# Rounding constant taken off on ScalarE, value bias added on TensorE, and two result buffers in a quantised attention stage

## What is computed

```python
def _dyn_quant(x):
    s = jnp.maximum(jnp.max(jnp.abs(x), axis=-1, keepdims=True) / 127.0, EPS)
    q = jnp.clip(jnp.round(x / s), -127.0, 127.0)
    return (q, s)
def _w8a8_linear(x, w, b):
    qx, sx = _dyn_quant(x)
    qw, sw = _quant_weight(w)
    y = jnp.einsum('bnc,oc->bno', qx, qw) * (sx * sw[:, 0])
    return y + b
...
q = _w8a8_linear(x, wq, bq)          # per head
k = (cond @ wk.T + bk)
v = (cond @ wv.T + bv)
scores = q k^T * inv_sqrt_d + mask
o = softmax(scores) @ v
return _w8a8_linear(o, wo, bo)
```

## Time and profile before

| | |
|---|---|
| runs | 4305.97, 4312.45, 4316.20 us; median 4312.45 |
| the profiled execution | 4308.22 us; span 4306.5 us; mean granted TensorE clock 0.948 of full speed |
| busy over the whole span | TensorE 3818.6 us (89%), VectorE 2617.0 (61%), ScalarE 1997.2 (46%), GpSimd 901.2 (21%) |
| quantised attention | from 16 us to 328.5 us of the span |
| in 140 to 160 us | ScalarE 18.38 of 20 us busy, VectorE 17.81, TensorE 15.39, GpSimd 2.51, granted clock 1.00 |
| gated attention | from about 3648 us to about 3950 us |

### The profile page before, as it was taken

One profiled execution on the slowest core, in us unless ns is written; L12 is line 12 of the kernel. 1 busy time (PEld: TensorE's weight loads), 2 busy tenths in 40 slices (PEclk: granted clock), 3 DMA queues, 4 the chain that ended last, 5 costly groups with the idle time before them and its releaser, 6 DMA issues. The chain is left out here.

```text
span 4306.5 us, 76239 instructions
## 1 busy us (share of the span) xinstructions
PE 3818.6 (89%) x26248; PEld 3246.2 (75%) x26248; DVE 2617.0 (61%) x5941; ACT 1997.2 (46%) x5211; POOL 901.2 (21%) x743
## 2 busy tenths in 40 slices
PE   6776999999998886999999999699989998898791
PEld 5655888888776775788888888588878887676670
DVE  7878999999577554555555555444434333777533
ACT  6885666666322443444433443333333332886140
POOL 1113333333101441000000000122322333111245
PEclk9997999999999997999999999899999999998695
DMA  2001000000002111111111111322223221003144
GB/s 72 18 13 47 1 0 0 0 0 1 25 22 76 44 56 64 52 38 40 41 38 36 38 40 40 100 75 70 72 66 105 75 74 59 16 15 93 58 135 129
DMA packets 149757, 209.49 MB, mean 49 GB/s; under 512 B 20800, under 2 KB 87648, under 8 KB 149216
## 3 DMA queue, kind: packets, MB, share of 16 engines
q1 hardware_dynamic: 142608, 187.14, 14.1%
q0 software_dynamic: 6864, 18.75, 1.6%
HBM read 178.18 MB, written 27.66 MB: 48 GB/s over the span
## 5 line engine op out<-in xcount | busy, mean ns | idle before, releaser
L1572 ACT ACTIVATE peer_tab<-peer_sims 128x128 f32<-128x128 f32 x1024 | 305.6, 393 | 0.0
L1579 POOL TENSOR_TENSOR peer_tab<-peer_sims 128x2048 f32<-128x2048 f32 x64 | 247.0, 3880 | 276.9 <-ACT peer_sims L1556 248.5
L1627 DVE SCALAR_TENSOR_TENSOR peer_tab<-peer_tab,peer_th 128x2048 f32<-128x2048 f32 x128 | 298.3, 2373 | 2.6 <-ACT peer_tab L1572 2.3
L1644 PE MATMUL bank<-ident,peer_tab 128*128 128x128 f32 x2048 | 247.9, 275 | 23.7 <-DVE peer_tab L1627 23.7
L1644 PEld LDWEIGHTS bank<-ident,peer_tab 128*128 128x128 f32 x2048 | 234.5, 142 | 37.1 <-DVE peer_tab L1627 24.6
L1694 PE MATMUL bank<-peer_wd,peer_hh 128*128 128x256 f32 x1024 | 246.3, 384 | 2.4 <-DVE peer_hh L1685 2.4
L1667 PE MATMUL bank<-peer_hT,peer_wg 128*128 128x256 f32 x1024 | 244.3, 382 | 0.0
L952 DVE TENSOR_TENSOR moe2a_b<-moe2a_a,moe2a_spread 128x512 f32<-128x512 f32 x104 | 78.6, 756 | 235.7 <-ACT moe2a_a L926 232.6
L1667 PEld LDWEIGHTS bank<-peer_hT,peer_wg 128*128 128x128 f32 x1024 | 195.8, 191 | 27.1
L952 DVE TENSOR_TENSOR moe2b_b<-moe2b_a,moe2b_spread 128x512 f32<-128x512 f32 x96 | 68.0, 708 | 234.6 <-ACT moe2b_a L926 232.9
L1694 PEld LDWEIGHTS bank<-peer_wd,peer_hh 128*128 128x128 f32 x1024 | 184.8, 190 | 30.9 <-DVE peer_hh L1685 7.4
(11 more groups left out here) (502 smaller groups left out, 10942.8 us busy)
## 6 DMA issues: line engine op xcount, KB each, us to landing
mha_wo<-mha_wo SPq DMA_DIRECT2D x128, 256.0 KB, 2.6
moe2b_spread<-moe_shares SPq DMA_DIRECT2D x48, 256.0 KB, 3.1
moe2a_spread<-moe_shares SPq DMA_DIRECT2D x40, 256.0 KB, 3.3
m_y_rows<-moe_y SPq DMA_DIRECT2D x79, 128.0 KB, 1.7
att_ctxT<-in_ctxT_dram SPq DMA_DIRECT2D x32, 256.0 KB, 2.6
lin_ctxT<-in_ctxT_dram SPq DMA_DIRECT2D x16, 256.0 KB, 2.6
ffn_in_gq<-in_ctxT_dram SPq DMA_DIRECT2D x16, 256.0 KB, 2.6
ffn_in_gq<-in_ctx_dram SPq DMA_DIRECT2D x16, 256.0 KB, 3.0
```

The source lines that it names most:

```text
L1572: i = nc.scalar.activation(tab[g][h][:, b * P:(b + 1) * P], sims[:, g, 1, h, :], ACT.Identity, bias=sims[:, g, 0, h, b:b + 1])
L1579: nc.gpsimd.tensor_tensor(out=tab[g][h][:].rearrange("p (a b) -> p a b", b=P), in0=sims[:, g, 1, h, :].unsqueeze(1).broadcast_to([P, NB, P ...
L1627: nc.vector.scalar_tensor_tensor(out=tab[g][h][:], in0=tab[g][h][:], scalar=th[:, g, h:h + 1], in1=tab[g][h][:], op0=ALU.is_ge, op1=ALU.mu ...
L1644: i = nc.tensor.matmul(TB[n % 2][:, j * P:(j + 1) * P], tab[g][h][:, blk * P:(blk + 1) * P], core.ident[:], start=(j == 0 and h == 0), sto ...
```

## The change

Four things are changed, three of them for the quantised layer alone.

The constant is no longer taken off by VectorE. The fp32 values with MAGIC still in them (xn, o) are turned by TensorE in fp32, and ScalarE's copy out of PSUM, an Identity with the column -MAGIC as bias, writes the bf16 integers. `xn_ready` and `on_ready` are raised by the additions of MAGIC. Since TensorE now reads xn itself, VectorE waits for the last turning before it writes xn. `o` becomes two buffers, one for a group, and the wait before it is written is for the turning two results back.

The value bias is added by TensorE: a matmul of a 16 x 128 tile of 1/16 with 16 equal rows of bv opens each bank of values. VectorE's addition goes.

GpSimd writes `fixed` (and the new tile) first and clears semaphores behind its first power operation. In the gated layer `fixed` and VectorE's wait for it are gone, and the copy of the result is an Identity with a bias of plain zero where it was a Copy.

```diff
@@ rows_dve
+            if some((t - 1) * 3 + INPUT // 2 + 1):
+                dve.wait_ge(filled[INPUT % 2], (t - 1) * 3 + INPUT // 2 + 1)
...
-            i.then_inc(norm_chain.sem, 1)
-            dve.wait_ge(norm_chain.sem, norm_chain.next())
-            if some((t - 1) * 3 + INPUT // 2 + 1):
-                dve.wait_ge(filled[INPUT % 2], (t - 1) * 3 + INPUT // 2 + 1)
-            nc.vector.scalar_tensor_tensor(out=qx[:].rearrange("p g d -> p (g d)"), in0=xn[:].rearrange("p g d -> p (g d)"), scalar=MAGIC,
-                                           in1=fixed[:, 1:2].broadcast_to([P, GU * D]), op0=ALU.subtract, op1=ALU.add).then_inc(xn_ready, 1)
+            i.then_inc(xn_ready, 1)
@@ input_pe
-                i = nc.tensor.transpose(F[:, c * UNIT + g * P:c * UNIT + (g + 1) * P], src[:, g, c * P:(c + 1) * P], idt[:])
+                i = nc.tensor.transpose(F[:, c * UNIT + g * P:c * UNIT + (g + 1) * P], xn[:, g, c * P:(c + 1) * P], core.ident[:])
@@ input_act
-            nc.scalar.activation(hT_of(par)[:].rearrange("p c t -> p (c t)"), FB[INPUT % 2][:].bitcast(BF16)[:, 0:C * UNIT],
-                                 ACT.Copy).then_inc(emptied[INPUT % 2], 1)
+            if is_int(t, 0):
+                act.wait_ge(fixed_set, 1)
+            nc.scalar.activation(hT_of(par)[:].rearrange("p c t -> p (c t)"), FB[INPUT % 2][:], ACT.Identity,
+                                 bias=fixed[:, 1:2]).then_inc(emptied[INPUT % 2], 1)
@@ values_pe
+        if quant and n == 0 and is_int(t, 0):
+            pe.wait_ge(fixed_set, 1)
+        if quant:
+            nc.tensor.matmul(F[:, 0:D], sixteenths[:], bv[0:16, :], start=True, stop=False)
         for c in range(C):
-            i = nc.tensor.matmul(F[:, 0:D], ctxT[par][:, c, n * P:(n + 1) * P], wvT[:, c, :], start=(c == 0), stop=(c == C - 1))
+            i = nc.tensor.matmul(F[:, 0:D], ctxT[par][:, c, n * P:(n + 1) * P], wvT[:, c, :], start=(c == 0 and not quant), stop=(c == C - 1))
@@ result_dve
+        elif some(n - 1):
+            dve.wait_ge(oT_filled, n - 1)
...
-        nc.vector.tensor_tensor(out=o[:], in0=o[:], in1=bv[:], op=ALU.add).then_inc(out_chain.sem, 1)
-        dve.wait_ge(out_chain.sem, out_chain.next())
...
+        nc.vector.scalar_tensor_tensor(out=o[g][:], in0=o[g][:], scalar=rso[:], in1=fixed[:, 0:1].broadcast_to([P, D]),
+                                       op0=ALU.mult, op1=ALU.add).then_inc(on_ready, 1)
-        if some(n):
-            dve.wait_ge(oT_filled, n)
-        nc.vector.scalar_tensor_tensor(out=oq[:], in0=o[:], scalar=MAGIC, in1=fixed[:, 1:2].broadcast_to([P, D]),
-                                       op0=ALU.subtract, op1=ALU.add).then_inc(on_ready, 1)
@@ result_pe, result_act
-            i = nc.tensor.transpose(F[:, c * P:(c + 1) * P], src[:, c * P:(c + 1) * P], idt[:])
+            i = nc.tensor.transpose(OB[g][:, c * P:(c + 1) * P], o[g][:, c * P:(c + 1) * P], core.ident[:])
-        nc.scalar.activation(oT[:].rearrange("p c t -> p (c t)"), F[:, 0:C * P], ACT.Copy).then_inc(oT_ready, 1)
+        nc.scalar.activation(oT[:].rearrange("p c t -> p (c t)"), OB[g][:, 0:C * P], ACT.Identity,
+                             bias=fixed[:, 1:2] if quant else 0.0).then_inc(oT_ready, 1)
@@ block.vector, block.gpsimd
-            dve.wait_ge(fixed_set, 1)
+            if quant:
+                dve.wait_ge(fixed_set, 1)
-            core.clear_stale(pool)
-            nc.gpsimd.memset(fixed[:, 0:1], MAGIC)
-            nc.gpsimd.memset(fixed[:, 1:2], 0.0).then_inc(fixed_set, 1)
+            if quant:
+                nc.gpsimd.memset(fixed[:, 0:1], MAGIC)
+                nc.gpsimd.memset(sixteenths[:], 0.0625)
+                nc.gpsimd.memset(fixed[:, 1:2], -MAGIC).then_inc(fixed_set, 1)
```

More of the change, by code:

```diff
@@ L2535, in head_attention_stage @@
     fixed = sb("fixed", [P, 2])
-    o = sb("o", [P, D])
+    o = [sb(f"o{i}", [P, D]) for i in range(GU)] if quant else [sb("o", [P, D])] * GU
     oT = sb("oT", [P, C, P], wdt)
@@ L2548, in head_attention_stage @@
     on_ready, oT_filled, oT_ready, y_ready, y_used = (sem(n) for n in ("on_ready", "oT_filled", "oT_ready", "y_ready", "y_used"))
-    out_chain = Chain(sem("out_chain"), GU * (7 if quant else 2))
+    out_chain = Chain(sem("out_chain"), GU * (5 if quant else 2))
     y_chain = Chain(sem("y_chain"), GU)
@@ L2554, in head_attention_stage @@
         sx, rsx = sb("sx", [P, GU]), sb("rsx", [P, GU])
-        qx, qf = sb("qx", [P, GU, D], BF16), sb("qf", [P, GU, D])
+        qf, sixteenths = sb("qf", [P, GU, D]), sb("sixteenths", [16, P])
         swq_col, bq_col = sb("swq_col", [P, C]), sb("bq_col", [P, C])
@@ L2560, in head_attention_stage @@
         cols_filled, cols_ready, hi_ready, lo_ready = sem("cols_filled"), sem("cols_ready"), sem("hi_ready"), sem("lo_ready")
-        so, rso, oq = sb("so", [P, 2 * GU]), sb("rso", [P, 1]), sb("oq", [P, D], BF16)
+        so, rso = sb("so", [P, 2 * GU]), sb("rso", [P, 1])
         mask = [sb(f"mask{i}", [P, GU, S]) for i in range(2)]
         qf_ready, xb_ready = sem("qf_ready"), sem("xb_ready")
-        norm_chain = Chain(sem("norm_chain"), 7)
+        norm_chain = Chain(sem("norm_chain"), 6)
     else:
@@ L2723, in input_pe @@
         F = fbank(pe, t, INPUT)
-        src, idt = (qx, core.identb) if quant else (xn, core.ident)
-        F = F[:].bitcast(BF16) if quant else F
         for c in range(C):
             for g in range(GU):
-                i = nc.tensor.transpose(F[:, c * UNIT + g * P:c * UNIT + (g + 1) * P], src[:, g, c * P:(c + 1) * P], idt[:])
+                i = nc.tensor.transpose(F[:, c * UNIT + g * P:c * UNIT + (g + 1) * P], xn[:, g, c * P:(c + 1) * P], core.ident[:])
         i.then_inc(filled[INPUT % 2], 1)
@@ L2962, in result_dve @@
                 dve.wait_ge(oT_filled, n)
-        i = nc.vector.tensor_tensor(out=o[:].rearrange("p (h d) -> p h d", d=HD), in0=sums[:, :, 0:HD],
+        elif some(n - 1):
+            dve.wait_ge(oT_filled, n - 1)
+        i = nc.vector.tensor_tensor(out=o[g][:].rearrange("p (h d) -> p h d", d=HD), in0=sums[:, :, 0:HD],
                                     in1=rsum[:].unsqueeze(2).broadcast_to([P, NH, HD]), op=ALU.mult)
@@ L2970, in result_dve @@
         dve.wait_ge(out_chain.sem, out_chain.next())
-        nc.vector.tensor_tensor(out=o[:], in0=o[:], in1=bv[:], op=ALU.add).then_inc(out_chain.sem, 1)
-        dve.wait_ge(out_chain.sem, out_chain.next())
-        nc.vector.tensor_reduce(out=s_, in_=o[:], axis=AX.X, op=ALU.max, apply_absolute_value=True).then_inc(out_chain.sem, 1)
+        nc.vector.tensor_reduce(out=s_, in_=o[g][:], axis=AX.X, op=ALU.max, apply_absolute_value=True).then_inc(out_chain.sem, 1)
         dve.wait_ge(out_chain.sem, out_chain.next())
@@ L2978, in result_dve @@
         dve.wait_ge(out_chain.sem, out_chain.next())
-        nc.vector.scalar_tensor_tensor(out=o[:], in0=o[:], scalar=rso[:], in1=fixed[:, 0:1].broadcast_to([P, D]),
-                                       op0=ALU.mult, op1=ALU.add).then_inc(out_chain.sem, 1)
-        dve.wait_ge(out_chain.sem, out_chain.next())
-        if some(n):
-            dve.wait_ge(oT_filled, n)
-        nc.vector.scalar_tensor_tensor(out=oq[:], in0=o[:], scalar=MAGIC, in1=fixed[:, 1:2].broadcast_to([P, D]),
-                                       op0=ALU.subtract, op1=ALU.add).then_inc(on_ready, 1)
+        nc.vector.scalar_tensor_tensor(out=o[g][:], in0=o[g][:], scalar=rso[:], in1=fixed[:, 0:1].broadcast_to([P, D]),
+                                       op0=ALU.mult, op1=ALU.add).then_inc(on_ready, 1)
     def result_pe(pe, t, g):
@@ L2989, in result_pe @@
         pe.wait_ge(on_ready, n + 1)
-        src, idt = (oq, core.identb) if quant else (o, core.ident)
-        F = OB[g][:].bitcast(BF16) if quant else OB[g]
         for c in range(C):
-            i = nc.tensor.transpose(F[:, c * P:(c + 1) * P], src[:, c * P:(c + 1) * P], idt[:])
+            i = nc.tensor.transpose(OB[g][:, c * P:(c + 1) * P], o[g][:, c * P:(c + 1) * P], core.ident[:])
         i.then_inc(oT_filled, 1)
@@ L3204, in unit_gp @@
         if is_int(t, -2):
+            core.clear_stale(pool)
             pool.wait_ge(weights_in, n_in)
```

## The result

The changed kernel takes 4321.88 us (median of 20 runs, 4309.36 to 4329.91), the kernel before 4308.80 us (20 runs, 4304.03 to 4316.20) in the same measurement: a ratio of 1.0027, 95% interval 1.0020 to 1.0035. It is slower by about 12 us, the forecast was no change at 4310, and the time lies above its range. The profiled execution of the changed kernel took 4312.29 us with a span of 4310.5; it is one of the quicker ones of its twenty.

The account below looks back on a forecast made before the run. No engine was full and three were close, so the order of waits decides. Loop +0.8, start -0.7, drain -1.5, gated -0.6 sum to -2.0 us: 4306.2 profiled, 4310 as median, range 4303 to 4320.

Parts of the forecast that it names:

- The residual addition: VectorE's addition in the quantised attention unit: would end by about 150.4, 1.1 us earlier.
- Attn x V: TensorE's matmuls in the quantised unit: would wait for pT alone and start 0.96 us earlier.
- the turn-taking: VectorE and GpSimd on SBUF: they alternate by instruction, so the residual addition gets in during GpSimd's mask subtraction.
- Rival (b): Quantised units: GpSimd keeps VectorE out until its bias addition is over; +7.5 us, 4320; chance 0.12.
- the term for the bias matmuls: TensorE in each quantised unit: two more matmuls cost 0.8 us, plus 0.1 for four changes of rows.
- The bound of 1.56: TensorE in each quantised unit: upper bound for the bias matmuls, 0.8 us plus four unhidden weight loads of 190 ns.
- rival (c): Quantised units: the bias matmuls expose all their weight loads; +6.6 us, 4319; chance 0.08.
- Rival (a): Quantised units: TensorE does not bind, its clock holds, units run at ScalarE's 17.70 us; -9.0 us, 4303; chance 0.18.
- Loop: All 13 quantised units: TensorE takes over from ScalarE; about +0.8 us, bounds -1.8 and +9.4.
- Start: Start of the quantised stage: constants come first, about -0.5 us; -0.7 together, 0 to -1.6.
- Drain: End of the quantised stage: TensorE waits less for the uncovered result chain; -1.5 us, 0 to -1.9.
- Gated stage: Entry of the gated stage: VectorE's 3.33 us wait for constants goes, but weights also bind; 0.6 us gained.

Follow-up runs that it names:

- e2: The changed kernel with the bias matmuls using 128 rows of 1/128 instead of 16 of 1/16; ratio to the kernel before 0.9983.
- e5: The changed kernel with the bias matmul last in the first value bank and first in the second, so both stand side by side; ratio 1.0001.
- e3: The changed kernel with the value bias added by VectorE as before and no bias matmul; ratio to the kernel before 0.9983.
- e7: The changed kernel with the value bias on VectorE and the input put back as before, leaving the result part; ratio to the kernel before 0.9972.
- e8: The changed kernel with the value bias on VectorE and the result put back as before, leaving the input part; ratio to the kernel before 0.9992.
- e9: The kernel before with only the value bias moved to TensorE, as matmuls of 128 rows; ratio to the kernel before 1.0023.
- e4: The kernel before with only the value bias moved to TensorE, as matmuls of 16 rows; ratio to the kernel before 1.0052.
- e1: The changed kernel once more, nothing edited, for a second profile; ratio to the kernel before 1.0035.
- e6: The changed kernel with 64 rows of 1/64 instead of 16 of 1/16 in the bias matmuls, same places; ratio to the kernel before 1.0014.

## Why the prediction was wrong

**Right: VectorE, the wait it ends, and ScalarE.** The residual addition now ends 155.35 - 146.38 = 8.97 us after the keys, against 10.68 in the earlier trace rows: 1.7 us earlier, where 1.1 was forecast. It did not have to take turns, since it starts 0.05 us before GpSimd; so the turn-taking that the forecast counted on was not put to the test. Attn x V is earlier by 11.07 - 10.11 = 0.96 us, and 0.96 was the forecast. The wait for the minimum is gone, and oT takes 0.59 to 0.62 us against 0.50 in the earlier trace rows. Rival (b) is out.

**Wrong: the term for the bias matmuls.** It was put at 0.8 + 0.1 us and measured 1.50, with 0.09 more ahead of the value groups. The 0.8 was right (e2: 0.81). The 0.1 for four changes of rows was 0.78. The bound of 1.56, with all four loads uncovered, was met (1.59), and so rival (c), to which the prediction gave 0.08, names what happened. TensorE's way from attn x V to the keys then came to 8.28 us; the forecast was 6.48 + 0.1 + 0.9 + 0.1 + 0.21 = 7.79, its 0.1 for oT counted in, so the unit would have been 10.11 + 7.79 = 17.90 and is 18.39.

The evidence that was chosen against the bound was the passage from the masks to the 64-row scores in the earlier trace rows, 0.30 us for each of four masks and the change together. That is an average over matmuls longer than those of the values, and it hides the step (from start to start the four take 0.42, 0.23, 0.22 and 0.32 us). The weight loads of the kernel before show it, in a view that was not read there (PEld in order of time):

```profile
153.09 1.60 PEld L2812 LDWEIGHTS bank<-att_wvT,att_ctxT 128*128 128x128 f32 x8
154.71 0.19 PEld L2864 LDWEIGHTS bank<-att_mask_hi,att_identr 128*128 128x128 f32 x1
...
155.93 0.64 PEld L2875 LDWEIGHTS bank<-att_km,att_qT 64*64 64x64 f32 x16 [0.35 <-issue]
```

The masks' loads run ahead of their matmuls (154.71 against 154.74). The first load for the scores starts with them, at 155.93, after 0.35 us without a load: the uncovered load stood in the trace. What the prediction set against (c), that loads of other shapes run beneath matmuls, holds here for the masks' 128 rows and not for the scores' 64. The rule that it took from the Trainium skill beside this term ("TensorE: Matmul & The Clock Gate", "Why this matters for your kernels"), that a matmul of few rows takes as long as one of all rows, is about the matmul. This case agrees on that (0.59 us for two of 16 rows that follow others of 16 rows, in e5, and 0.59 for two of 128, in e2) and shows that the price lies in what stands next to it.

**Rival (a), half right.** Its outcome, units at ScalarE's pace and no falls, is what e2, e3 and e7 show: 17.56 to 17.62 us against its 17.70, ratios of 0.9972 to 0.9983. That is 7 to 12 us, where it gave 9. Its reason holds as far as counting goes: 4, 4, 5 and 8 falls in the four kernels in which VectorE takes the constant off the result (before, e8, e9, e4), none to two in the others. Those falls come behind waits of TensorE for the result of 1.6 to 1.8 us; in the others that wait is 0.8 to 1.3 us, and 1.5 in one unit of each that has the bias on TensorE. But not every such wait brings one: the kernel before has seven of 1.6 us and more in its thirteen units and four falls. Why the clock falls behind some of them was not tested. In the changed kernel this rival fell to the bias term.

**The sum, for the profiled execution.** Loop: +6.5 us (key matmuls from 50.35 to 285.83 before, 51.47 to 293.48 now), where +0.8 was forecast and +9.4 the upper bound. Without its one fall it is +3.3: nine units longer by 0.55, four that had a fall shorter by 0.45. The fall of 6.8 us cost 3.2, a term that the prediction lacked; one of 3.4 us cost 1.3 in e1 and in e6, against 1.0 before. The prediction's own terms give +0.94 rather than +0.8 here (nine times 0.06 and four times 0.1), and rival (b)'s keys come at 159.76 rather than 159.84; neither decides anything. Start: +1.1 where -0.7 was forecast. The row (start of the stage on VectorE):

```profile
16.32 0.75 DVE L2606 BATCH_NORM_STATS2 att_stats<-x 128x6 f32<-128x256 f32 x2 [0.74 <-POOL att_fixed L3270]
```

The constants come 0.66 us earlier than in the earlier trace rows, and the first keys 0.87 us, but the first units pay for the bias too (the value groups take 44.78 to 47.87, 3.09 us). The first unit has a mean granted clock of 1.00 here and 0.88 before, so the clock hides part of the loss. Drain: -2.4 from the last keys to the end, where -1.5 was forecast; e4, where only the bias addition is gone from the result chain, shows -2.1 as well, and the mean granted clock of the drain is 0.87 in these two and 0.78 before, so the profile does not tell the chain from the clock. Gated stage, VectorE and GpSimd:

```profile
3655.28 0.75 DVE L2606 BATCH_NORM_STATS2 att_stats<-x 128x6 f32<-128x256 f32 x2 [0.32 <-PEq L1182]
```

```profile
3664.04 0.20 POOL L3201 TENSOR_TENSOR att_hmask<-att_hmask 128x4 f32<-128x4 f32 x1 [4.74 <-DMA att_keep<-in_keep_dram]
```

The wait of 3.33 us for the constants is gone and has become a longer wait for the weights, 4.74 us instead of 1.28 in the earlier trace rows: of the 0.6 us that was forecast, nothing came at the start. The stage then ends 2.3 us earlier against its start, but that cannot be put down to the change: the two other kernels with the old code there show +0.2 (e4) and -2.3 (e9), and the other nine with the new code lie between -2.0 (e2) and +1.1 (e6). So no gain is shown in the gated stage. Together 6.5 + 1.1 - 2.4 - 2.3 = +2.9; the span grew by 4.0, and the remaining 1.1 lies in stages that the change leaves alone.

**What stays open.** The medians differ by 13.1 us, the two profiled executions by 4.1. The forecast of -2.0 us was set on a median of three, 4312.45, and would be 4306.8 on the median of twenty. Rival (c) had +9.4 in the loop, which shows +3.3 without the fall, so it is in part luck that the median came out near its 4319. A run of the changed kernel can be 20 us longer than another, and e1's 15 us more lay to a third in the stage and to two thirds outside it. So of the 13 us the runs show 5 to 10 in the stage. The rest is spread over stages with the same code, and whether the change has a part in that is not known. The unit ahead of the thirteen has a mean granted clock of 0.74 to 0.90 in ten of the thirteen profiles, and of 1.00 in those of the kernel before, the changed kernel and e9. In e1, e5 and e6 it is some 4 us longer for it, which is part of their stage's end in the table. No run tells why.

## What to carry to other kernels

Before giving TensorE a small matmul, look at the weight loads on either side of it: where the number of rows changed, the load stood uncovered, 0.195 us for each change here. 128 rows of 1/128 in place of 16 rows of 1/16 took that away, and the small matmuls side by side took half of it away. Work that is moved to another engine is priced against that engine's spare time after the whole change: the same bias was free next to the earlier residual addition (e2) and a loss without it (e9). A change of several parts is best sized part by part, since here one part carried the gain, one the loss, and two, the input and the second buffer, did nothing that shows. The new starts of the two stages were not tried by themselves.

## What the runs showed of the hardware

Of these fp32 weights, a group of 128 rows behind one of 16 or 64 rows, or the other way round, starts its first load with its own matmuls, after 0.33 us without a load (0.17 us at the first change; e6 the same as the changed kernel). Behind weights of the same number of rows it starts 0.21 us ahead of its own matmuls (128 rows in e2, 16 rows in e5). A fall of the clock that lasted 3.4 us made a unit 1.0 us longer in the kernel before, 1.3 us in e1 and 0.5 to 0.8 us in e4; the falls of 6.8 us in the changed kernel and in e1 made it 3.2 us longer.
